# First cross-attention of a two-layer block on one core: scores laid out with keys on partitions, and the softmax's maxima and mask brought in as matrix products

## The reference

```python
x = x + tanh(g_xattn[0]) * attention0(layernorm(x), ctx)   # 16 heads of 8, mask the same for all batches and heads
x = x + tanh(g_ffn[0])   * ternary_ffn(layernorm(x))       # Hadamard rotation, 4-bit activations, ternary weight
x = x + tanh(g_xattn[1]) * attention1(layernorm(x), ctx)   # 16 heads of 64, a mask for each batch
x = x + tanh(g_ffn[1])   * moe(x)                          # 32 experts of width 64, best 4, and a shared one
# attention0, for head h:  softmax(where(mask, q @ k.T / sqrt(8), -max_float)) @ v ; then the output projection
```

## Time and profile before

| what | value |
|---|---|
| median of 3 runs | 279.56 us (279.52 to 281.11) |
| profiled execution | 278.56 us; span 276.7 us, mean granted clock 0.984 |
| PE busy | 254.6 us (92%), 1909 matmuls |
| DVE busy | 207.6 us (75%) |
| ACT busy | 187.1 us (68%) |
| POOL busy | 138.4 us (50%) |

### The profile page before, as it was taken

How to read it: one execution, slowest core, us unless ns; L and a number is a source line. 1 busy time by engine, 2 the same in 40 slices (tenths; PEclk the granted TensorE clock), 3 DMA queues, 4 the chain that set the end, 5 groups by cost and what they waited for, 6 DMA issues and landing times. The chain is left out here.

```text
span 276.7 us, 6465 instructions
## 1 busy us (share of the span) xinstructions
PE 254.6 (92%) x1909; PEld 202.6 (73%) x1909; DVE 207.6 (75%) x593; ACT 187.1 (68%) x395; POOL 138.4 (50%) x209
## 2 busy tenths in 40 slices
PE   7798999999698999997999999999979998789994
PEld 5475766677566687786777888777767776789993
DVE  3989679778987697788578777777798514786673
ACT  3379779878677687784866767678776553666462
POOL 7305710204125075754465485448847794926380
PEclk9979999999799999999999999999999999999998
DMA  6568375200032656644574766766532041200530
GB/s 200 192 178 284 131 267 137 55 4 2 0 70 60 142 121 148 135 104 107 135 184 113 179 174 171 194 162 160 141 82 60 24 136 38 85 33 28 189 112 19
DMA packets 25984, 32.88 MB, mean 119 GB/s; under 512 B 4000, under 2 KB 18144, under 8 KB 25824
## 3 DMA queue, kind: packets, MB, share of 16 engines
q1 hardware_dynamic: 25520, 32.27, 43.4%
q10 hardware_dynamic: 432, 0.22, 0.3%
HBM read 14.32 MB, written 3.47 MB: 64 GB/s over the span
## 5 line engine op out<-in xcount | busy, mean ns | idle before, releaser
L1220 PE MATMUL bank<-ident,probs 128*128 128x128 f32 x512 | 79.7, 279 | 3.1 <-ACT probsT L757 1.3
L1220 PEld LDWEIGHTS bank<-ident,probs 128*128 128x128 f32 x512 | 59.3, 143 | 20.5 <-issue 15.9
L596 POOL TENSOR_SCALAR probs<-probs,rsum 128x512 f32<-128x512 f32 x64 | 44.2, 693 | 49.7 <-DVE rsum L945 49.6
L757 ACT ACTIVATE probsT<-bank 128x512 f32<-128x512 f32 x77 | 45.7, 593 | 24.3 <-PE bank L1220 24.3
L936 DVE CUSTOM_DVE_ANT_0 masked<-bank,mask 128x512 f32<-128x512 f32 x64 | 43.8, 684 | 18.7 <-PE bank L1352 17.0
L744 ACT ACTIVATE probs<-masked,neg_max 128x512 f32<-128x512 f32 x64 | 44.4, 722 | 8.0 <-DVE neg_max L936 6.0
L1379 PE MATMUL bank<-probsT,val 128*32 128x256 f32 (+1 forms) x512 | 46.6, 384 | 0.9 <-ACT mixT L768 0.9
L749 ACT ACTIVATE probs<-masked,neg_max 128x512 f32<-128x512 f32 x64 | 46.0, 719 | 1.6 <-DVE neg_max L936 1.6
L936 DVE CUSTOM_DVE_ANT_0 masked<-bank,shared 128x512 f32<-128x512 f32 x64 | 42.4, 685 | 5.0 <-PE bank L1345 4.9
L952 DVE COPY probsT<-bank 128x512 f32<-128x512 f32 x51 | 34.9, 684 | 6.7 <-PE bank L1220 6.4
L1379 PEld LDWEIGHTS bank<-probsT,val 128*32 128x32 f32 (+1 forms) x512 | 24.9, 123 | 18.0 <-issue 5.1
(11 more groups left out here) (244 smaller groups left out, 546.8 us busy)
## 6 DMA issues: line engine op xcount, KB each, us to landing
k_both<-k_low SPq DMA_DIRECT2D x32, 128.0 KB, 2.6
k_both<-k_high SPq DMA_DIRECT2D x32, 128.0 KB, 2.7
q<-q_split SPq DMA_DIRECT2D x32, 128.0 KB, 2.4
probsT<-staged_gate SPq DMA_DIRECT2D x32, 128.0 KB, 3.0
q<-q_split SPq DMA_DIRECT2D x32, 64.0 KB, 2.0
parts<-staged_k SPq DMA_DIRECT2D x7, 256.0 KB, 2.7
w_flat<-in_w SPq DMA_DIRECT2D x1, 1536.0 KB, 8.0
staged_k<-k_high SPq DMA_DIRECT2D x2, 512.0 KB, 3.2
```

The lines of the kernel that those rows point to most:

```text
L596: pool.tensor_scalar(p, p, rsum[:, u % NCOL:u % NCOL + 1], 1.0, ALU.mult, ALU.mult).then_inc(normed, 1)
L757: act.activation(probsT[:, k.m % 2, h, :, qt * P:qt * P + P], turn_bank[u % 2][:, :].rearrange("p (k q) -> p k q", q=P), ACT.Copy).then_in ...
L1220: ins = pe.transpose(dst[0:rows, t * P:t * P + P], src, ident[:, :])
```

## The change

Block 0 and attention1 keep their form. For blocks 1 to 7 (units 8 to 63, `CROSS_AT` = 8) the scores are computed twice.

- First as before, queries on partitions, up to 15 steps ahead (`CROSS_LEAD`), two a step from step 1 until that lead is reached. The scan only leaves the negated maxima in `nm`; its full output goes to `unread`.
- After a block's eight scans DVE splits the maxima into high and low and transposes them in squares of 32 (`gather`). SP writes them to DRAM and reads them back into one or the other free row of each head's queries, a DMA for each head and part (`stage_rows`). The free rows come from the fourth product (low by low), which is dropped: keys have ones there, queries the maxima.
- Then in step t PE computes half of one head's scores with keys on partitions, 2 x 128 keys by 256 queries (`cross`): the mask comes in as the identity times the transposed mask in bf16, over 512 columns, and two matmuls of 256 columns add keys times queries with the maxima. ACT takes the exponential straight from the bank to `probsT` (`exp_crossed`). There are no transposes and no copies for these units.
- Batch 1's layer norm and projections come earlier (`LN01_AT` = 0; keys at step 3, queries at 6, values at 8). ACT copies the odd units of block 0, DVE the even ones.
- New fills and conversions ahead of the first step: a row of ones and one of zeros to DRAM, the transposed mask, the identity in bf16.

```diff
-LN01_AT = 6
+LN01_AT = 0
...
+
+CROSS_AT = BLOCKS[1].first
+CROSS_LEAD = 15
+
+
+def crosswise(u):
+
+    return CROSS_AT <= u < L1_AT
+
+
+def scores_at(u):
+
+    return max(u - CROSS_LEAD, 1 + (u - CROSS_AT) // 2) if crosswise(u) else u - LEAD
+
+
+S_ORDER = sorted(range(TOTAL), key=lambda u: (scores_at(u), crosswise(u), u))
+S_NUMBER = {u: n for n, u in enumerate(S_ORDER)}
+S_AT = {t: [u for u in S_ORDER if scores_at(u) == t] for t in range(-LEAD, TOTAL)}
+GATHERS = {scores_at(k.end - 1) + 1: k for k in BLOCKS[1:8]}
+
+
+def scored_block(k):
+
+    return 1 + max(S_NUMBER[u] for u in range(k.first, k.end))
+
+
+def turned_before(u):
+
+    return u if u < CROSS_AT else u - L1_AT + CROSS_AT
+
+
+def probs_slot(u):
+
+    return u % (NP - 1) if u < L1_AT else (u - L1_AT) % NP
...
-    for n, name in enumerate(("kn", "qn", "v0")):
-        plan.setdefault(LN01_AT + 7 + n, []).append((name, 1))
+    for o, name in ((3, "kn"), (6, "qn"), (8, "v0")):
+        plan.setdefault(LN01_AT + o, []).append((name, 1))
...
-    plan.setdefault(LN01_AT + 5, []).append(("ln", 0, 1))
+    plan.setdefault(LN01_AT + 4, []).append(("ln", 0, 1))
...
 def on_act(u):
 
-    if u < L1_AT:
-        return u % 5 in (1, 3, 4)
     return u % 2 == 1 or u in MORE_ON_ACT
...
+            def stage_rows(k):
+
+                n = k.m - 1
+                sp.wait_ge(gathered, n + 1)
+                sp.dma_start(staged_rows[k.m % 2], rows_turned[:, :]).then_inc(rows_staged, 16)
+                sp.wait_ge(rows_staged, 16 * (n + 1))
+                if k.m >= 3:
+                    sp.wait_ge(crossed, BLOCKS[k.m - 2].end - 1 - CROSS_AT)
+                src = staged_rows[k.m % 2].rearrange("(i l h t) c -> l h t i c", i=4, l=4, t=NQ)
+                for h in range(4):
+                    for low in range(2):
+                        p = 32 * h + 4 * low + 3
+                        sp.dma_start(q0[p:p + 1, k.m % 4, h, :].bitcast(F32).rearrange("p (t i c) -> p t i c", t=NQ, i=4),
+                                     src[low, h:h + 1]).then_inc(rows_loaded[k.m % 2][h], 16)
 
             def stack_k0(k):
...
+            sp.wait_ge(late_ready, 4)
+            sp.dma_start(staged_k[:, :, 3, :].bitcast(F32).rearrange("b p k -> p b k"),
+                         ones_row.unsqueeze(1).to_broadcast([P, B, SK])).then_inc(ld["rows"], 16)
+            sp.dma_start(staged_q[:, :, 3, :].bitcast(F32).rearrange("b p q -> p b q"),
+                         zero_row.unsqueeze(1).to_broadcast([P, B, SQ])).then_inc(ld["rows"], 16)
             stage_k0(0)
             stage_q0(0)
-            sp.wait_ge(late_ready, 3)
+            sp.wait_ge(late_ready, 5)
+            sp.wait_ge(ld["rows"], 32)
...
             stage_k0(1)
+            stage_rows(BLOCKS[1])
             stage_q0(1)
+            stage_rows(BLOCKS[2])
             for k in BLOCKS[4:8]:
                 stack_k0(k)
                 stack_q0(k)
+                if k.m >= 5:
+                    stage_rows(BLOCKS[k.m - 2])
+            stage_rows(BLOCKS[6])
+            stage_rows(BLOCKS[7])
...
+            publish_late(pool.memset(ones_row, 1.0))
+            publish_late(pool.memset(zero_row, 0.0))
...
+            pool.tensor_scalar(maskT[:, :, :], m0T_u8[:, :, :], FAR, -FAR, ALU.mult, ALU.add).then_inc(maskT_ready, 1)
...
+            def exp_crossed(u):
+
+                k, h, half = unit(u)
+                act.wait_ge(crossed, u - CROSS_AT + 1)
+                if k.m >= 2:
+                    act.wait_ge(mixed, k.m - 1)
+                act.activation(probsT[:, k.m % 2, h, 2 * half:2 * half + 2, :],
+                               turn_bank[u % 2][:, :].rearrange("p (k q) -> p k q", q=SQ),
+                               ACT.Exp, scale=float(k.depth) ** -0.5).then_inc(cross_exped, 1)
...
+                n, o = S_NUMBER[u], turned_before(u)
+                dve.wait_ge(scored, n + 1)
+                if crosswise(u):
+                    c = u - k.first
+                    if n >= 2:
+                        dve.wait_ge(maxed, n - 1)
+                    dve.tensor_tensor_reduce(out=unread[:, n % 2, :], in0=score_bank[n % 2][:, :], in1=mask0[:, qt, :],
+                                             scale=-1.0, scalar=3.0e38, op0=ALU.add, op1=ALU.min,
...
+            def gather(k):
+
+                n = k.m - 1
+                high, low = row_parts[:, 0:8], row_parts[:, 8:16]
+                dve.wait_ge(maxed, scored_block(k))
+                step(dve.tensor_copy(high, nm[:, k.m % 2, :]))
+                step(dve.tensor_tensor(low, nm[:, k.m % 2, :], high.bitcast(F32), ALU.subtract))
+                if n:
+                    dve.wait_ge(rows_staged, 16 * n)
+                dve.transpose(rows_turned[:, :], row_parts[:, :].bitcast(F32)).then_inc(gathered, 1)
...
+                    dve.tensor_copy(ident_b[:, :], ident[:, :]).then_inc(ident_ready, 1)
+                    dve.memset(row_parts[:, :].bitcast(F32), 0.0)
...
+            def cross(u):
+
+                k, h, half = unit(u)
+                dst = turn_bank[u % 2]
+                if half == 0:
+                    pe.wait_ge(rows_loaded[k.m % 2][h], 32 * ((k.m + 1) // 2))
+                if u < CROSS_AT + 2:
+                    pe.wait_ge(maskT_ready, 1)
+                    pe.wait_ge(ident_ready, 1)
+                    pe.wait_ge(copied[u % 2], CROSS_AT // 2)
+                else:
+                    pe.wait_ge(cross_exped, u - CROSS_AT - 1)
+                pe.matmul(dst[:, :], ident_b[:, :], maskT[:, 2 * half:2 * half + 2, :], start=True, stop=True, skip_group_check=True)
+                for n in range(2):
+                    c = (2 * half + n) * P
+                    ins = pe.matmul(dst[:, n * SQ:n * SQ + SQ], k0[:, k.m % 4, c:c + P], q0[:, k.m % 4, h, :],
+                                    start=False, stop=True, skip_group_check=True)
+                ins.then_inc(crossed, 1)
...
```

More of the change, by code:

```diff
@@ L378, in build @@
         turned = sem("turned")
+        gathered = sem("gathered")
+        rows_staged = sem("rows_staged")
+        rows_loaded = [[sem(f"rows_loaded{i}{h}") for h in range(4)] for i in range(2)]
+        crossed = sem("crossed")
+        cross_exped = sem("cross_exped")
         copied = [sem("copied0"), sem("copied1")]
@@ L480, in stack_k0 @@
                 sp.wait_ge(k_staged[k.b], 32)
-                if k.m >= 4:
-                    sp.wait_ge(scored, BLOCKS[k.m - 4].end)
+                if k.m == 4:
+                    sp.wait_ge(scored, scored_block(BLOCKS[0]))
+                elif k.m > 4:
+                    sp.wait_ge(crossed, BLOCKS[k.m - 4].end - CROSS_AT)
                 sp.dma_start(k0[:, i, :].bitcast(F32),
@@ L517, in stack_k @@
                 sp.wait_ge(*freed(("k", k.m)))
-                sp.wait_ge(scored, BLOCKS[k.m - NKQ].end)
+                sp.wait_ge(scored, scored_block(BLOCKS[k.m - NKQ]))
                 for h in range(2):
@@ L789, in job @@
                     if name == "k":
-                        act.wait_ge(scored, BLOCKS[k.m - NKQ].end)
+                        act.wait_ge(scored, scored_block(BLOCKS[k.m - NKQ]))
                         high = k1_high[:, k.m % NKQ, :]
@@ L1150, in _ @@
                     dve.wait_ge(mask_ready[1], B * NQ)
-                if 0 <= t + LEAD - 1 < TOTAL:
-                    mask_max(t + LEAD - 1)
+                for u in S_AT.get(t - 1, ()):
+                    mask_max(u)
+                if t in GATHERS:
+                    gather(GATHERS[t])
                 if L1_AT <= t + LEAD - 3 < TOTAL:
@@ L1156, in _ @@
                     job(j)
-                if 0 <= t - 1 < TOTAL and not on_act(t - 1):
+                if 0 <= t - 1 < TOTAL and not on_act(t - 1) and not crosswise(t - 1):
                     copy_turned(t - 1)
@@ L1410, in attend @@
             def attend(t):
-                if 0 <= t + LEAD < TOTAL:
-                    scores(t + LEAD)
+                for u in S_AT.get(t, ()):
+                    scores(u)
                 for j in PLAN.get(t, ()):
@@ L1508, in lay_out @@
         w00T[:, i, :] = np.repeat(f[n][0:32].T, 4, axis=1)
+        w00T[:, i, 3::4] = 0.0
     new["w00T"] = w00T
@@ L1538, in lay_out @@
     row = np.arange(P)
-    cols[:, COL["lo_k"]] = np.where(row % 2, -1.0, 0.0)[:, None]
-    cols[:, COL["lo_q"]] = np.where(row // 2 % 2, -1.0, 0.0)[:, None]
+    cols[:, COL["lo_k"]] = np.where(row % 4 == 1, -1.0, 0.0)[:, None]
+    cols[:, COL["lo_q"]] = np.where(row % 4 == 2, -1.0, 0.0)[:, None]
     cols[:, COL["neg_half"]] = -0.5
```

109 lines of the change are left out of this document (72 added, 37 removed).

## The result

The changed kernel takes 297.24 us (median of 4 runs, 294.0 to 299.84) beside 279.88 for the kernel before: a ratio of 1.057, interval 1.048 to 1.067, 17.4 us slower. The slowest of the four runs, over 1.5% above the fastest, is left out of the ratio, by which the loss is 16.0 us. The profiled execution took 296.84 us (span 295.1, mean granted clock 0.970). The forecast was 281.5 and its range ended at 290.

The account below looks back on a forecast made before the run. PE, ACT and DVE were taken as nearly full in the first layer; 10.5 - 16.1 + 3.5 + 2.0 + 1.2 + 1.0 = +2.1 us on the profiled 278.56, forecast 281.5, range 278 to 284 (8 in 10: 273.5 to 290).

Parts of the forecast that it names:

- the term -16.1: From step 8 to the turn of unit 64: PE's own work, 60.3 us against 76.4, if nothing else waits.
- quantisation +2.0: First layer: the quantisation still holds the scans and with them PE's scores, +2.0 us.
- ACT +1.2: Steps 49 to 57, without scores: ACT's 0.6 us a unit outlasts PE's 0.47, +1.2 us.
- The opening: Up to step 8: doubled scores and scans and the maxima's relay bring it at 36.2 instead of 25.73, +10.5 us.
- SP's queue: DMA issues at 8.1 us a block; block 4's loads stand behind the maxima, PE waits at step 17, +3.5 us.
- The rival's condition: SP's relay sets the pace if issues exceed about 0.46 us or landings 2.5: about +10 us, 291; chance 0.18.
- the three new matmuls: PE, each unit of blocks 1 to 7: mask and two 256-column matmuls take 0.47 us, replacing transposes of 0.45.
- the rival of dearer matmuls: PE's new matmuls take 0.61 us, weight loads not hidden: 7.8 us more, so 289; chance 0.10.
- the activation: ACT, units 8 to 63: exponential and copy become one activation from PSUM, 0.6 us instead of 1.08 a unit.
- the second layer: After 102 us, from unit 64's turn on: PE is full and the change leaves these steps as they are.
- The clock: The stall at step 17 may bring the lower clock back, while that at 74 may go: +1.0 us, bounds 0 and 3.
- the clock rival: PE, half idle in steps 1 to 8, stays at 1.2 GHz and falls again at the stall: 284; within forecast's 0.45.

Follow-up runs that it names:

- experiment 5: Changed kernel without the maxima's way through DRAM, first scores six steps ahead, one a step: 280.04 us, 1.002 of the kernel before.
- experiment 2: Changed kernel without the maxima's way through DRAM and without first scores, scans and gathers of blocks 1 to 7: 274.35 us, 0.982 of the kernel before.
- 7 to 10: Batch 0's ternary layer left out of the changed kernel, experiment 2, experiment 5 and the kernel before: 291.59, 269.82, 272.76 and 275.84 us.
- experiment 9: Experiment 5 without batch 0's ternary layer, attention1's first keys and queries at steps 46 and 47, its turn of x earlier: 272.76 us, 0.972 of the kernel before.
- 1: Changed kernel without the maxima's write and reads through DRAM; scores, scans and gathers stay: 291.39 us, 1.043 of the kernel before.
- experiment 12: Changed kernel with 22, 12 and 5 useless identity matmuls on PE ahead of steps 17, 52 and 53: 297.06 us, 1.060 of the kernel before.
- 7: Changed kernel without batch 0's ternary layer (projection, rotation, quantisation and product): 291.59 us, 1.049 of the kernel before.

## Why the prediction was wrong

**The step that failed** is the term -16.1: "Sum 60.3, against 76.4: -16.1 us, if nothing else waits". It took PE's own work as the bound from step 8 to turn 64. Divide the stretch at step 40. Of the 8.2 us of jobs only 1.2 stand before that step (eleven matmuls of 128 columns in the changed kernel's trace), and 7.0 behind it. So the same prices give for steps 8 to 40: 32 x 0.47 + 32 x 0.22 + 4 x 1.89 + 1.2 = 30.8, and experiment 5 measured 33.4 there. For steps 40 to 64: 24 x 0.47 + 8 x 0.22 + 3.8 + 3 x 1.89 + 7.0 = 29.5, and the changed kernel took 41.6, experiment 2, with no first scores at all, 39.3. The sum was 2.6 us short in one half without the relay, and 12.1 in the other. The terms "quantisation +2.0" and "ACT +1.2" are all that I had allowed for there; 8.9 us more were missing. I had read the stretch 65 to 78 for its clock and its DVE and had added up each job's price, and never followed from which job the next one waits. Busy time in that stretch, before (63.70 to 102.10) and changed (78.50 to 120.10):

```profile
63.70:102.10 38.40, 33.79 (x270) 25.94 (x271) 31.81 (x94) 28.37 (x55) 13.41 (x19) 0.96 0.30 67
```

```profile
78.50:120.10 41.60, 33.85 (x236) 24.54 (x239) 21.26 (x70) 20.91 (x43) 12.17 (x18) 0.88 0.29 63
```

DVE has 10.6 us less to do and ACT 7.5, PE has 34 matmuls less, and the stretch is 3.2 us longer. The chain of dependent jobs in it takes 28.6 us before and 28.7 in experiment 2, in which all first scores and scans of blocks 1 to 7 are gone. That relieved engines don't shorten this stretch is shown by experiments 2 and 5, and that the chain has a part in it by 7 to 10. The chain isn't all of it: with the chain cut the stretch still takes 34.4 us in experiment 9, with PE idle for only 2.9, so the sum was too low there even without the chain's waits. Two things stay open. What sets the 34.4 to 34.9 us of either form with the chain cut was not tried. And the chain took longer in the changed kernel (31.3), in 5 (31.2, from 58.88 to 90.06) and in 1 (33.1, from 71.02 to 104.14) than the 28.6 before; with the clock held up in experiment 12 it took 29.9 (75.10 to 104.96), so that about half of the changed kernel's excess of 2.7 may be clock, and the rest isn't settled.

**The opening** was the right mechanism, mis-sized: +12.4 against +10.5. I had DVE alone at 9.7 and the relay at 0.8 more; in the changed kernel's profile they are 10.6 and 1.8. The working has a slip: its own terms (28.1, six scans of 0.61, 1.1) put the last score at 32.9, not 33.6, and with the projection step 8 at 34.0 by DVE alone. DVE's list was short of a second gather (0.6), of the values' copy (0.65) and of one copy of a turned unit (0.6), and its first gather took 1.5 us, not 0.5. Its timeline, changed kernel:

```profile
27.40 0.58 DVE L1058 CAST k_both<-val 128x8 fp32r<-128x8 f32 x1
28.02 0.65 DVE L1059 TENSOR_TENSOR k_both<-val,k_both 128x8 fp32r<-128x8 f32 x1
...
36.16 0.17 DVE L1058 CAST k_both<-val 128x8 fp32r<-128x8 f32 x1
```

**SP's queue**: the stall at block 4 was foreseen and came, 5.1 us where 3.5 was the term. Its parts were off in both senses: reads 0.65, not 0.43; the first write landed at 35.4, not 33.5; the second, 2.0, was near the 2.1 expected. The rival's condition (over 0.46 us an issue) was met, its outcome (waits at every block) was not: PE waited for the rows once, 1.8 us at step 8. SP did fall behind (the last read of block 3's maxima was issued by 62.3, forecast 53.6), but PE was later still (step 24 at 61.30, forecast 55.1). In the Trainium skill (DMA: Bandwidth & Descriptors, Rules for kernel authors) many small transfers are to be made one, since under 64 KB one pays mostly overhead; the page's Anatomy of one DMA puts the fixed cost at about 2.0 us, for DMAs issued from GpSimd. The second write's 2.0, issued from SP, agrees with that figure; the first's 6.5 and the third's 3.5 don't, and what cost most here was the issuing of the reads, 5.2 us a block.

**Right by its price**: the three new matmuls (0.70 a step less the score's 0.22 to 0.23 is 0.47 to 0.48, forecast 0.47; the rival of dearer matmuls falls), the activation (0.598, forecast 0.6), and the second layer, unchanged from turn 64 on within 0.4 us.

**The clock**: +1.0 was allowed for. The granted clock did fall after each long wait, but by experiment 12 it is worth about that 1.0 in the profile, and nothing that the ratio shows. The opening is the place that the clock rival named. There the changed kernel's profile was at 1.00 from 18 to 24, and in the three others, at 0.50 to 0.58, PE was through with its own work 0.7 to 2.1 us later (37.03 to 38.40 against 36.28), without the 1.8 of waiting for rows. No run was made to hold the clock up there.

**The size of the error**: +18.0 at turn 64 instead of +2.1. Of the 15.9 between them the opening made 1.9; steps 8 to 40 made 6.1 (40.4 against 30.8 and the 3.5 of the stall), 1.6 of it the longer stall and 2.6 what is missing without a relay too; steps 40 to 64 made 8.9 (41.6 against 29.5 and 3.2); and 1.0 for the clock is to be taken off.

## What to carry to other kernels

Before engines' busy time is turned into a gain, cut the stretch at the points where one stage hands over to the next, and for each part measure the chain of dependent jobs as well as the busiest engine: the saving is bounded by the longer of the two. Look too for loops of two engines over two banks: in experiment 2 such a loop kept the step at 0.70 us though a third of PE's work in it was gone. Here a stage with 10.6 us of DVE's work and 7.5 of ACT's taken away became 3.2 us longer. Work done ahead must be paid for at the start, where here no other work covered it, and a value that makes a round trip through DRAM should be costed by what stands ahead of it in the queue and by the number of its issues, not by its bytes.

## What the runs showed of the hardware

- A read that lands on one partition took 0.63 to 0.68 us to issue (eight in 5.01 to 5.46), one onto 32 partitions 0.44 (four in 1.77).
- A 16 KB write to DRAM was seen landed after 2.0, 3.5 and 6.5 us, the longest behind 2.0 MB of weights and 0.75 MB of keys. In experiment 12, issued 1.2 us later behind the same transfers, it took 3.6.
- A matmul of the 128x128 identity by itself in 32-bit floats takes 0.23 us (44 of them in 9.99, with two records each), where four transposes of the same size take 0.45 together.
- The first gather's two small DVE operations took 0.58 and 0.65 us in the changed kernel (0.17 and 0.63 in experiment 12, 0.72 and 0.54 in 7), all later ones 0.17; why was not tried.
- With the same program up to there, the granted clock from 18 to 24 us was 1.00 in one profile, 0.58 in two and 0.50 in one.
